# The wide attentions' output product with the output matrix as weights, in a decoder on one Trainium2 core

## The reference

```python
def _mha(x, y, ..., causal):
    xn, yn = _ln(x, lnx_g, lnx_b), _ln(y, lny_g, lny_b)
    q, k, v = (einsum with wq, wk, wv)              # 16 heads of 32
    a = softmax(einsum('bhsd,bhtd->bhst', q, k) * D ** -0.5)
    if causal: a = a * mask
    o = einsum('bhst,bhtd->bhsd', a, v)             # to (16, 256, 512)
    x_out = x + o @ li1_w + li1_b                   # <- the product the change is about
    h = gelu(_ln(x_out, ln3_g, ln3_b) @ li2_w + li2_b)
    return x_out + h @ li3_w + li3_b
x = _ln(xx, ln1_g, ln1_b)
x = x + _mha(x, x, a1..., causal=True)
x = _ln(x, ln2_g, ln2_b)
return x + _mha(x, ee, a2..., causal=False)
```

## Time and profile before

| | us |
|---|---|
| median of three runs | 3404.22 (3403.7 to 3407.45) |
| the profiled execution | 3408.74 |
| its span, first to last instruction | 3407.0 |
| stretch of the s5a_ loop and its end, 2180 to 2640 of the span | 460 |
| stretch of the s5c_ loop and its end, 2765 to 3025 | 260 |

### The profile page before, as it was taken

One profiled execution on the slowest core, in us unless ns is written; L12 is line 12 of the kernel. 1 busy time (PEld: TensorE's weight loads), 2 busy tenths in 40 slices (PEclk: granted clock), 3 DMA queues, 4 the chain that ended last, 5 costly groups with the idle time before them and its releaser, 6 DMA issues. The chain is left out here.

```text
span 3407.0 us, 52663 instructions
## 1 busy us (share of the span) xinstructions
PE 2564.8 (75%) x16155; PEld 1876.6 (55%) x16155; DVE 2209.6 (65%) x4477; ACT 1528.5 (45%) x4269; POOL 890.7 (26%) x1242
## 2 busy tenths in 40 slices
PE   4888888861695999989622978799998789976085
PEld 2666666650694666656412765466665556655075
DVE  4999999961124777767675323588886479955144
ACT  4666666620123777755320122477775344432011
POOL 4344333425451000022202100111110133311654
PEclk8888888875796999999855569799998989997588
DMA  9200000001662000000003000000000000000166
GB/s 355 108 0 0 0 0 0 0 1 38 187 191 66 1 0 0 1 6 0 7 0 52 8 0 0 15 1 0 0 0 8 15 1 0 0 8 1 46 196 193
DMA packets 107646, 128.11 MB, mean 38 GB/s; under 512 B 30266, under 2 KB 80133, under 8 KB 103429
## 3 DMA queue, kind: packets, MB, share of 16 engines
q1 hardware_dynamic: 98308, 107.59, 10.7%
q0 software_dynamic: 9216, 19.02, 1.6%
HBM read 69.16 MB, written 57.41 MB: 37 GB/s over the span
## 5 line engine op out<-in xcount | busy, mean ns | idle before, releaser
L669 DVE TENSOR_TENSOR_SCAN s_state<-s_decay,s_state 128x4096 f32<-128x4096 f32 x32 | 278.0, 8687 | 33.9 <-ACT s_decay L467 33.9
L565 PE MATMUL s_ysumP<-s_state,ident 128*128 128x256 f32 x1024 | 289.0, 436 | 1.6 <-DVE s_state L679 1.6
L1163 ACT ACTIVATE s5a_prob<-s5a_scoreP,s5a_nmax 128x256 f32<-128x256 f32 x512 | 235.6, 475 | 65.4 <-DVE s5a_nmax L1337 65.1
L565 PEld LDWEIGHTS s_ysumP<-s_state,ident 128*128 128x128 f32 x1024 | 219.2, 225 | 35.7 <-DVE s_state L679 1.9
L510 PE MATMUL s_bcP<-s_bc,s_sel 96*128 96x256 bf16 x768 | 151.5, 338 | 103.9 <-DVE s_state L679 90.3
L1163 ACT ACTIVATE s2s_prob<-s2s_scoreP,s2s_nmax 128x128 f32<-128x128 f32 (+1 forms) x512 | 208.6, 424 | 45.5 <-DVE s2s_nmax L1335 44.3
L467 ACT ACTIVATE s_decay<-s_delta,s_aneg 128x255 f32<-128x255 f32 x512 | 210.0, 494 | 33.1 <-DVE s_delta L646 32.9
L2692 POOL DMA_INDIRECT parts<-m_y,m_to x160 | 153.6, 960 | 148.1 <-DVE m_y L2783 123.1
L1337 DVE TENSOR_REDUCE s5a_nmax<-s5a_scoreP 128x4 f32<-128x1024 f32 x128 | 156.6, 1223 | 44.4 <-PE s5a_scoreP L1258 41.8
L2861 PE MATMUL m_turnP<-ident,m_xin 128*128 128x128 f32 x160 | 32.9, 289 | 196.6 <-DMA m_w<-in_m_w 196.4
L510 PEld LDWEIGHTS s_bcP<-s_bc,s_sel 96*128 96x128 bf16 x768 | 82.3, 117 | 173.2 <-DVE s_state L679 122.6
(11 more groups left out here) (572 smaller groups left out, 6401.3 us busy)
## 6 DMA issues: line engine op xcount, KB each, us to landing
sorted<-blank SPq DMA_DIRECT2D x32, 1105.0 KB, 28.1
m_w<-in_m_w SPq DMA_DIRECT2D x120, 256.0 KB, 3.2
m_xin<-sorted SPq DMA_DIRECT2D x80, 130.0 KB, 2.3
m_row<-parts SPq DMA_DIRECT2D x32, 256.0 KB, 5.2
m_w<-in_m_w SPq DMA_DIRECT2D x40, 128.0 KB, 3.1
s_mats<-s_scratch SPq DMA_DIRECT2D x4, 1024.0 KB, 17.0
parts<-m_y,m_to POOLq DMA_INDIRECT x160, 3.3
sorted<-m_row,m_idx POOLq DMA_INDIRECT x128, 2.3
```

Source lines behind the costliest of these rows:

```text
L565: ins = nc.tensor.matmul(ysumP[:, c, :], ident[:], state[s][:, c, n, :], start=(n == 0), stop=(n == NS - 1))
L669: nc.vector.tensor_tensor_scan(cells, flat(decay[c]), cells, 0.0, ALU.mult, ALU.add).then_inc(S["scanned"], 1)
L1163: ins = nc.scalar.activation(prob[i][:, h, a:b], scoreP[i][:, h, a:b], ACT.Exp, bias=nmax[:, p % 4, h, r:r + 1], accum_out=den[s][:, r, 2 ...
```

## The change

For WIDE only, the product L is turned round. The output matrix is loaded as weights, four pieces, and all 256 rows of oT stream against each, so the result stands as columns by rows. ScalarE reads it from PSUM with the bias as a per-partition operand into a new SBUF tile outT. A new item M turns outT back with two transposes into the same PSUM bank, and VectorE adds that to the residual. VectorE's addition of the bias row is gone. bo is now one column, loaded as such.

```diff
-                     tag + "bo": w("li1_b").reshape(1, C), tag + "w1": w("li2_w").reshape(C, 4, P),
+                     tag + "bo": w("li1_b").reshape(C, 1), tag + "w1": w("li2_w").reshape(C, 4, P),
 # attend_self
-            AT_B = {1: [("R0", -1)], 2: [("R1", -1)]}
+            AT_B = {1: [("R0", -1)], 2: [("R1", -1)], 4: [("M", -1)]}
 # attend_cross
-        AT = {0: [("L", -2), ("Q1", 0)], 1: [("T", 1), ("K", 1)], ...
+        AT = {0: [("L", -2), ("Q1", 0)], 1: [("M", -2), ("T", 1), ("K", 1)], ...
 # both, TensorE (itemP in attend_self)
+                elif n == "M":
+                    for g in range(TB):
+                        ins = nc.tensor.transpose(itemA[:, g * P:g * P + P], outT[:, g * P:g * P + P], ident[:])
+                elif WIDE:
+                    for c in range(OT):
+                        ins = nc.tensor.matmul(itemA[:, 0:L], wo[:, c, :], oT[:, c, :], start=(c == 0), stop=(c == OT - 1))
 # what make waits for, attend_cross
-                before = {..., "T": [("L", b - 2), ("V", b)], "R0": [("T", cap(b + 3)), ("L", b)], ...
+                before = {..., "M": [("L", b + 1)], "T": [("M" if WIDE else "L", b - 2), ("V", b)],
+                          "R0": [("T", cap(b + 3)), ("M" if WIDE else "L", b)], ...
 # both, ScalarE
+                if n == "L":
+                    wait(ac, made["M"], b)
+                    nc.scalar.activation(outT[:], itemA[:, 0:L], ACT.Identity, bias=bo[:, 0:1]).then_inc(used[n], 1)
+                    return
 # both, VectorE
-                if n == "L":
+                if n in ("L", "M"):
                     nc.vector.tensor_tensor(rows(dst, b), rows(base, b), itemA[...], ALU.add
-                                            ).then_inc(used["L"], 1)
-                    if not bias:
-                        ve.wait_ge(used["L"], b + 1)
-                        nc.vector.tensor_tensor(rows(dst, b), rows(dst, b), bo[...], ALU.add).then_inc(S["biased"], 1)
+                                            ).then_inc(used[n], 1)
```

More of the change, by code:

```diff
@@ L1115, in take @@
             def take(n, b, s):
-                if n in ("L", "R0", "R1"):
+                if n in ("R0", "R1", "M") or (n == "L" and not WIDE):
                     return
                 ac.wait_ge(made[n], b + 1)
+                if n == "L":
+                    wait(ac, made["M"], b)
+                    nc.scalar.activation(outT[:], itemP[:, 0:L], ACT.Identity, bias=bo[:, 0:1]).then_inc(used[n], 1)
+                    return
                 if n == "T":
@@ L1188, in _ @@
             o_take(NB - 1, 3)
+            if WIDE:
+                take("L", NB - 1, 1)
         @block.tensor
@@ L1317, in _ @@
             pv(NB - 1, 1, QUADS - 1)
-            for n in (("R0", "R1", "L") if WIDE else ("R0", "L")):
+            for n in (("R0", "R1", "L", "M") if WIDE else ("R0", "L")):
                 make(n, NB - 1, 1)
@@ L1397, in _ @@
             recip(NB - 1, 1)
-            for n in (("R0", "R1", "L") if WIDE else ("R0", "L")):
+            for n in (("R0", "R1", "M") if WIDE else ("R0", "L")):
                 take(n, NB - 1, 1)
-            ve.wait_ge(S["biased"], NB)
+            ve.wait_ge(used["M"] if WIDE else S["biased"], NB)
 def attend_cross(nc, ident, dram, tag, hat, base, dst, D, ln, bias, ctx_ln, affine=None, add_to=None):
@@ L1456, in attend_cross @@
         itemB = sc.ps("itemB", [P, 512])
-        names = ["loaded", "biased", "sel_ready", "zeroed", "bias_ready", "cstep", "step", "pool_step", "staged", "scores", "maxed",
+        names = ["loaded", "sel_ready", "zeroed", "bias_ready", "cstep", "step", "pool_step", "staged", "scores", "maxed",
                  "subbed", "exped", "turned", "probT_ready", "pv", "densed", "o_out", "recip", "expanded", "yT_mm", "yT_ready",
                  "chat_ready", "y_ready", "kbd_ready"]
-        items = ["T", "Q0", "Q1", "K", "V", "R0", "R1", "L"] if WIDE else ["T", "Q0", "K", "V", "R0", "L"]
+        items = ["T", "Q0", "Q1", "K", "V", "R0", "R1", "L", "M"] if WIDE else ["T", "Q0", "K", "V", "R0", "L"]
         QL = "Q1" if WIDE else "Q0"
@@ L1502, in attend_cross @@
         else:
[L1503 removed]
+            loads += [(bo[:], dram[tag + "bo"])]
         if ln:
@@ L1684, in _ @@
                 o_take(NB - 1, 1, u)
+            if WIDE:
+                take("L", NB - 2, 0)
+                take("L", NB - 1, 1)
         @block.tensor
@@ L1782, in _ @@
             pv(NB - 1, 1, 3)
-            make("L", NB - 2, 0)
-            for n in (("R0", "R1", "L") if WIDE else ("R0", "L")):
+            for n in (("L", "M") if WIDE else ("L",)):
+                make(n, NB - 2, 0)
+            for n in (("R0", "R1", "L", "M") if WIDE else ("R0", "L")):
                 make(n, NB - 1, 1)
@@ L1827, in take @@
             def take(n, b, s):
[L1828 removed]
+                if n not in (("M", "R0", "R1") if WIDE else ("L", "R0")):
                     return
                 ve.wait_ge(made[n], b + 1)
[L1831 removed]
+                if n in ("L", "M"):
                     nc.vector.tensor_tensor(rows(dst, b), rows(base, b), itemA[:, 0:TB * P].rearrange("p (g c) -> p g c", g=TB),
[L1833 to L1837 removed]
+                                            ALU.add).then_inc(used[n], 1)
                     return
@@ L1864, in _ @@
             recip(NB - 1, 1)
-            take("L", NB - 2, 0)
-            for n in (("R0", "R1", "L") if WIDE else ("R0", "L")):
+            take("M" if WIDE else "L", NB - 2, 0)
+            for n in (("R0", "R1", "M") if WIDE else ("R0", "L")):
                 take(n, NB - 1, 1)
-            wait(ve, S["biased"], 0 if bias else NB)
+            ve.wait_ge(used["M" if WIDE else "L"], NB)
 def heads32(w, np):
```

30 lines of the change are left out of this document (18 added, 12 removed).

## The result

The change is slower: ratio 1.0196 (1.0177 to 1.0216), a median of 3473.57 us (3468.12 to 3478.32) against 3405.84 on the same chip, 68 us more. The profiled execution took 3468.12, its span 3466.3, 59 more than before. That profiled difference is smaller because stages ahead of the change happened to run shorter, as the tile view shows: first and last start of three tiles in each kernel (line, engine, operation, tile, count, ns least/median/most, first to last start).

A forecast was written before the change was run, and what follows sets the result against it. The s5c_ cycle, TensorE from L to the scores of slot 2, then VectorE from maximum to oT (17.11 us a batch), was taken as the bound. 38 + 12 + 2 + 1 = 53 us slower, median 3457, range 3430 to 3476.

The forecast's parts named there:

- all the signs named for it: In s5c_: T waits 2 to 3 us, period about 20, maximum waits over 3, clock about 0.9; s5a_ period within 0.2.
- The wait of T: s5c_: T waits for VectorE's addition of M, 2.72 and 3.2 us in turn over 13 batches, 38 us.
- The clock: s5c_: TensorE's clock falls behind the new wait in eight of 13 batches at 1.5 us, 12 us; bounds nothing and 21.
- The ends: End of s5c_: the last two L followed by ScalarE's read and two transposes, the last M on VectorE; 2 us.
- s5a_: The s5a_ loop has room for M and stays as it was, 0 (bounds -2 and +4); +1 us for its end.
- The bias addition off the cycle: s5c_: removing VectorE's bias addition, 0.42 to 1.31 us a batch, is worth nothing, as it lies beside TensorE's 8.45 us.
- L, ScalarE's read, M: s5c_: turned L costs zero difference, ScalarE's 0.56 us read is hidden, M's two transposes by themselves 0.3 us a batch.
- The clock stays up: Rival, s5c_: new waits of 2.3 to 3 us leave TensorE's clock alone, 41 us slower, 3445; chance 0.25.
- VectorE is the bound: Rival, VectorE's slots in s5c_ and s5a_: bias additions come back as time, 11 us faster, 3393; chance 0.06.
- The round trip is absorbed: Rival, s5c_: T is ready late for another reason, so only M's 0.3 us counts, 3404 to 3412; chance 0.05.

The follow-up runs named there:

- filler_half: The change with four unused matmuls put between M and the waiting T in the 13 batches that have both; ratio 1.0135 against the kernel before.
- cross_only: The kernel before with the turned product and M in attend_cross alone, attend_self left as before; ratio 1.0207 against the kernel before.
- filler_two: The change with two unused matmuls put between M and the waiting T in the 13 batches that have both; ratio 1.0131 against the kernel before.
- self_only: The kernel before with the turned product and M in attend_self alone, attend_cross left as before; ratio 0.9998 against the kernel before.
- nobias: The kernel before with VectorE's additions of the bias row left out in both attentions, nothing else changed; ratio 1.0008 against the kernel before.
- m_last: The change with M moved on TensorE behind the turn and product of slot 1, T waiting only for ScalarE's read of L; ratio 1.0017 against the kernel before.
- reorder: The kernel before with the preceding batch's product and turn moved ahead of L and Q1 in attend_cross; ratio 0.9969 against the kernel before.
- early: The change with VectorE's addition of M moved ahead of maximum, difference and sums of slot 1; ratio 1.0060 against the kernel before.

## Why the prediction came out as it did

I forecast 3457 and the median was 3474, inside the range of 3430 to 3476 but only 2 us below its upper end. The mechanism was right, and all the signs named for it came; one term of the sum was less than half of what it should have been.

- *The wait of T:* 38 us forecast, at 2.72 and 3.2 in turn. T starts 2.75 and 3.07 later, filler_half prices it at 37 us. The alternation is there. The L87 behind which I had looked for it took 0.93 beside GpSimd's copy in the batch shown, and ended VectorE's list of slot 0 late enough for its maximum to start 0.36 behind the end of the scores; in the batch before it took 0.91, but the maximum then still waited 0.15 for the scores. No run isolates this.
- *The clock:* 12 us forecast, eight of 13 batches at 1.5, with 13 x 1.65 = 21 as upper bound. It was 28.5 (25.6 in cross_only): 13 batches at 2.0 to 2.2. This is the step that failed, in both its factors. The number rested on the waits ahead of L, which had cost nothing 13 times of 14; in filler_two's trace idle times of that length ahead of T cost in nine of 13. And the 1.65 was no bound: it came from one batch, in which only part of the work behind the wait ran slowly, while in the change it can be all of T to the scores of slot 2 and more (4.60 + 1.82 against 2.52 + 1.13, 2.8 us, in the batch shown). The Trainium skill (TensorE: Matmul & The Clock Gate, A second HAM failure mode: psum-queue depth-cycling) tells of a kernel in which short pauses of TensorE between groups of matmuls make its clock fall and return over and over. The trace agrees, 13 times of 13 in the change. I had weighed that with every batch paying, and for how many pay it was the better guide here.
- *The ends:* 2 us in s5c_ forecast. From the last s5c_sub to the first s5n_act it was 28.1 and is 30.7, 2.6 more; the stretch has 0.6 more ahead of that. In filler_half these ends are 29.2, 1.1 more, so some 1.5 of the 2.6 is the clock again: the last L took 3.58 against 1.97. *s5a_:* +1 forecast, +0.6 in the trace; the medians of self_only and before are 1 us apart, within the interval of -5 to +3.
- *The bias addition off the cycle:* right, nobias 1.0008 (0.9995 to 1.0020). *L, ScalarE's read, M:* 0.11 us a batch together, by m_last, where M's 0.3 is partly hidden and not paid in full.
- *Rivals:* "The clock stays up" (3445) is what filler_half makes of the change, +46 us; without the filler it is false. "VectorE is the bound" becomes true only in reorder. "The round trip is absorbed" falls with early: 1.12 us of delay, 1.10 us of period.

The parts measured are 37 + 28.5 + 2.6 = 68.1, against 68.6 us of the stretch. The first two come from the same traces as the stretch, so that they nearly add up to it is no further check; the check on 28.5 is TensorE's own rows. That the time lies inside the range is in part luck: no bound from which the range was made allowed the clock more than 21.

## What to carry to other kernels

Before an item is split in two in an engine's queue, look at what its second half shares with the item behind it, here one PSUM bank: a wait for another engine's read is free or a full round trip according to where that read stands in the other engine's list. Put such an item where the next user of the bank comes late. Time saved on an engine counts only once the other part of the cycle has been shortened, so look for work that is ready early and can fill the wait that closes the cycle.

## What had not been expected of the hardware

In the kernel before, the idle times ahead of L cost TensorE its clock once in 14, and that one was 1.92 us; twelve of 1.55 and one of 1.03 cost nothing. But ahead of T idle times of 0.63 and 0.95 us lost it in two batches of 13, 1.49 and 1.81 in nine, and 2.3 to 2.7 in all 13, with 0.50 of the full clock granted from 2818 to 2823, behind such a wait. And the same 1.03 us ahead of the last L left it at 1.97 us in five kernels and went with 3.39 and more in four others. So a price per wait taken from one place of a kernel did not hold at another place of the same kernel.
